# Delta-rule stages of a two-layer vision transformer on Trainium2: table switches, projections, inverse rows and the output product placed anew

## What is computed

```python
def step(S, inp):                       # one token; S is 16x16 for each head and image
    qt, kt, vt, at, gkt = inp
    Sp = S * jnp.exp(gkt)[..., None]
    u = jnp.einsum('bhk,bhkv->bhv', at, Sp) + vt
    S = Sp + jnp.einsum('bhk,bhv->bhkv', kt, u)
    o = jnp.einsum('bhk,bhkv->bhv', qt, S)
    return (S, o)
...
q, k, v = silu(x @ Wq), l2norm(silu(x @ Wk)), silu(x @ Wv)
log_f = jax.nn.log_sigmoid(x @ Wf)
gamma = -jax.nn.sigmoid(x @ Wgamma)
a = k * gamma * exp(log_f)
```

## Time and profile before

| what | value |
|---|---|
| median of 3 runs | 1997.47 us (1995.56 to 2000.2) |
| the profiled execution's own time | 1989.77 us |
| its span, first to last instruction | 1988.0 us |
| mean granted clock of TensorE | 0.857 |
| busy share of the span: TensorE, VectorE, ScalarE, GpSimd | 86%, 56%, 33%, 16% |
| first instruction of the delta stage k = 0 | 1303.05 us |
| start of k = 1, 2, 3 | 1321.4, 1348.1, 1392.3 us |
| start of k = 8, 9, 10 | 1687.3, 1743.8, 1789.5 us |
| first instruction after the last delta stage (ScalarE, L1324) | 1819.19 us |

### The profile page before, as it was taken

The page is one execution under the profiler, slowest core; times in us unless marked ns, Lnnn a source line. Parts: engine busy times, 40 slices in busy tenths (PEclk is TensorE's granted clock), DMA queues, the critical chain, the costliest instruction groups (busy, mean ns, idle before and its releaser), DMA issues. The chain is left out here.

```text
span 1988.0 us, 51796 instructions
## 1 busy us (share of the span) xinstructions
PE 1708.2 (86%) x22689; PEld 1517.3 (76%) x22689; DVE 1108.5 (56%) x2379; ACT 656.6 (33%) x1347; POOL 314.5 (16%) x284
## 2 busy tenths in 40 slices
PE   4677786799999999999999999876888888757589
PEld 4466675579988999989999999745877777756468
DVE  3655555674545555455555465566445555543885
ACT  3334534433322233232223232163333333223142
POOL 0232232520000000000000000052322223200530
PEclk9888988899999999999999999877666656655579
DMA  4100000100100000000101000100000000001001
GB/s 135 60 2 1 0 0 1 67 22 1 43 1 22 22 22 22 22 22 1 44 1 43 1 1 1 36 1 2 4 4 4 3 4 4 4 4 48 1 11 41
DMA packets 10070, 36.01 MB, mean 18 GB/s; under 512 B 3056, under 2 KB 6152, under 8 KB 7304
## 3 DMA queue, kind: packets, MB, share of 16 engines
q1 hardware_dynamic: 9864, 32.96, 4.8%
HBM read 30.47 MB, written 2.49 MB: 17 GB/s over the span
## 5 line engine op out<-in xcount | busy, mean ns | idle before, releaser
L1042 ACT ACTIVATE hidden<-bank,moe_b 128x512 f32<-128x512 f32 (+1 forms) x320 | 213.3, 668 | 537.1 <-PE bank L934 524.5
L951 PE MATMUL bank<-moe_w2h,hidden_hi 128*128 128x256 f32 x1216 | 345.7, 284 | 0.0
L951 PE MATMUL bank<-moe_w2l,hidden_hi 128*128 128x256 f32 x1216 | 344.0, 283 | 0.0
L951 PE MATMUL bank<-moe_w2h,hidden_lo 128*128 128x256 f32 x1216 | 343.9, 283 | 0.0
L934 PE MATMUL bank<-x_hi,moe_w1h 128*128 128x512 f32 (+1 forms) x640 | 243.8, 381 | 2.9 <-ACT hidden L1042 2.8
L934 PE MATMUL bank<-x_lo,moe_w1h 128*128 128x512 f32 (+1 forms) x640 | 242.5, 379 | 0.0
L934 PE MATMUL bank<-x_hi,moe_w1l 128*128 128x512 f32 (+1 forms) x640 | 242.0, 378 | 0.0
L951 PEld LDWEIGHTS bank<-moe_w2h,hidden_hi 128*128 128x128 f32 x1216 | 233.1, 192 | 6.0 <-DVE residual L1076 4.3
L1076 DVE SCALAR_TENSOR_TENSOR residual<-bank,gates,residual 128x256 f32<-128x256 f32 x152 | 73.4, 484 | 290.4 <-PE bank L951 290.4
L951 PEld LDWEIGHTS bank<-moe_w2l,hidden_hi 128*128 128x128 f32 x1216 | 233.2, 192 | 1.2
L951 PEld LDWEIGHTS bank<-moe_w2h,hidden_lo 128*128 128x128 f32 x1216 | 233.2, 192 | 0.0
(11 more groups left out here) (287 smaller groups left out, 3357.3 us busy)
## 6 DMA issues: line engine op xcount, KB each, us to landing
moe_w<-in_moe_w SPq DMA_DIRECT2D x16, 1024.0 KB, 4.8
patches<-in_patches SPq DMA_DIRECT2D x8, 864.0 KB, 4.6
out<-residual SPq DMA_DIRECT2D x19, 128.0 KB, 1.7
ffn_w<-in_ffn_w SPq DMA_DIRECT2D x2, 1024.0 KB, 6.4
att_w<-in_att_w SPq DMA_DIRECT2D x1, 1536.0 KB, 5.9
delta_w<-in_delta_w SPq DMA_DIRECT2D x1, 1280.0 KB
tok_w<-in_tok_w SPq DMA_DIRECT2D x1, 768.0 KB, 4.1
delta_wvf<-in_delta_wvf SPq DMA_DIRECT2D x1, 272.0 KB
```

The lines of the kernel that those rows point to most:

```text
L951: mm = nc.tensor.matmul(bank[4 + n % 3][:, 0:D], left, right, start=(i == 0), stop=(i == len(passes) - 1))
L1042: nc.scalar.activation(H[:, i % 4, 0:n], bank[i % 4][:, 0:n], ACT.Relu, bias=b1[:, x, f:f + 1]).then_inc(acted, 1)
```

## The change

Only `delta_stage` is changed.

- **ScalarE.** Three table loads a stage become two. Sigmoids come first, under one set: each value tile's Relu and Abs are followed at once by its sigmoid, then all four sigmoids of q and k. After `first_back(1)` comes the other set, then `forget_logs`, the two paddings and `inverse_norms`, ahead of the solution copies.
- **TensorE.** `project(0)` and `project(1)` stand right behind the values, `project(2)` and `project(3)` between the first halves. `key_norm(0)` and `key_norm(1)` move up behind `remainder(0)` and `remainder(1)`. `output` is called twice, with half of the lanes each; the first half goes into banks 2 and 3, the second into 0 and 1. `inverse_out(0)` moves ahead of `score(0)`, and `inverse_out(1)` ahead of `score(1)`.
- **VectorE.** All values and all silus come before row 5; `with_values(0)` before `log_forget`; rows 7 to 13 before the low parts of the output; `weigh(2)` and `weigh(3)` right behind row 15, `weigh(4)` and `weigh(5)` behind row 17, and the last two behind row 18.

```diff
@@ score, p == 0
-                        pe.wait_ge(o_lo, 2)
+                        pe.wait_ge(o_lo, 4)
@@ output
-            def output():
+            def output(j):
...
-                pe.wait_ge(u2_back, 4)
-                for p in range(IP):
+                pe.wait_ge(u2_back, 2 * (j + 1))
+                if j == 0 and c is not None:
+                    pe.wait_ge(v_out, 2)
+                for p in (2 * j, 2 * j + 1):
...
-                                    mm = nc.tensor.matmul(bank[s][32 * g:32 * g + 32, ts], UB[half(s), lane, :],
+                                    mm = nc.tensor.matmul(bank[2 - 2 * j + s][32 * g:32 * g + 32, ts], UB[half(s), lane, :],
@@ TensorE's list
             low_part(0)
             low_part(1)
-            first_half(0)
             project(0)
-            first_half(1)
             project(1)
             low_part(2)
-            remainder(0)
+            first_half(0)
             project(2)
             low_part(3)
-            remainder(1)
             project(3)
             low_part(4)
+            first_half(1)
+            remainder(0)
+            key_norm(0)
+            remainder(1)
+            key_norm(1)
             second_half(0)
             decay(0)
             second_half(1)
             decay(1)
-            key_norm(0)
-            key_norm(1)
-            output()
+            output(0)
             decay(2)
+            output(1)
+            inverse_out(0)
             score(0)
             decay(3)
-            inverse_out(0)
+            inverse_out(1)
+            score(1)
             decay(4)
-            score(1)
             decay(5)
-            inverse_out(1)
+            score(2)
             decay(6)
-            score(2)
             decay(7)
             inverse_out(2)
             score(3)
@@ ScalarE: high_out now takes (j, s), one copy of half the lanes for both m
-            nc.scalar.preload_act_table_set("natural_log_exp_and_others")
+            nc.scalar.preload_act_table_set("sigmoid_and_others")
             for p in range(IP):
                 forget_parts(p)
-            forget_logs()
-            nc.scalar.preload_act_table_set("sigmoid_and_others")
-            sigmoid_values(0)
-            sigmoid_values(1)
+                sigmoid_values(p)
+            sigmoid(0)
+            sigmoid(1)
             first_back(0)
-            sigmoid(0)
-            sigmoid_values(2)
-            first_back(1)
-            sigmoid(1)
-            sigmoid_values(3)
-            padded(0)
             sigmoid(2)
-            padded(1)
             sigmoid(3)
             for i in range(len(spans)):
                 low_high(i)
+            first_back(1)
             nc.scalar.preload_act_table_set("natural_log_exp_and_others")
+            forget_logs()
+            padded(0)
+            padded(1)
+            inverse_norms()
             solution(0)
             decay(0)
             solution(1)
             decay(1)
-            inverse_norms()
-            high_out(0)
-            high_out(1)
+            high_out(0, 0)
+            high_out(0, 1)
             decay(2)
+            high_out(1, 0)
+            high_out(1, 1)
+            inverse_back(0)
             decay(3)
-            inverse_back(0)
+            inverse_back(1)
             decay(4)
             decay(5)
-            inverse_back(1)
             decay(6)
             decay(7)
             inverse_back(2)
@@ VectorE: low_out takes (j, s) too, one subtraction; weigh waits for o_done 2
             for t in range(1, 5):
                 inverse_row(t)
-            log_forget()
-            inverse_row(5)
+            for p in range(IP):
+                values_of(p)
             silu_of(0)
-            values_of(0)
-            values_of(1)
             silu_of(1)
-            values_of(2)
-            values_of(3)
-            with_values(0)
             silu_of(2)
-            with_values(1)
             silu_of(3)
             gate_parts()
             step_scale()
-            for t in range(6, 10):
+            inverse_row(5)
+            with_values(0)
+            log_forget()
+            inverse_row(6)
+            bounded(0)
+            with_values(1)
+            bounded(1)
+            for t in range(7, 14):
                 inverse_row(t)
-            bounded(0)
-            bounded(1)
-            for t in range(10, 13):
-                inverse_row(t)
-            low_out(0)
-            low_out(1)
-            inverse_row(13)
+            for j in range(2):
+                for s in range(2):
+                    low_out(j, s)
             inverse_row(14)
             weigh(0)
             weigh(1)
             inverse_row(15)
+            weigh(2)
+            weigh(3)
             unit_key(0)
             unit_key(1)
             inverse_row(16)
-            weigh(2)
-            weigh(3)
             inverse_row(17)
+            weigh(4)
+            weigh(5)
             inverse_row(18)
-            for b in range(4, CB):
-                weigh(b)
+            weigh(6)
+            weigh(7)
```

More of the change, by code:

```diff
@@ L1616, in second_half @@
                 mm.then_inc(u2_done, 1)
-            def output():
+            def output(j):
                 if y is None:
                     return
-                pe.wait_ge(u2_back, 4)
-                for p in range(IP):
+                pe.wait_ge(u2_back, 2 * (j + 1))
+                if j == 0 and c is not None:
+                    pe.wait_ge(v_out, 2)
+                for p in (2 * j, 2 * j + 1):
                     for m in range(HALVES):
-                        ts = slice((IP * m + p) * SEQ, (IP * m + p + 1) * SEQ)
+                        ts = slice((2 * m + p % 2) * SEQ, (2 * m + p % 2 + 1) * SEQ)
                         for e in range(2):
@@ L1765, in padded, with high_out @@
                                      by_half(images(xl_c[:, m, nxt, :].bitcast(F32))), ACT.Copy).then_inc(in_lo, 1)
-            def high_out(s):
+            def high_out(j, s):
                 if y is None:
                     return
[L1770 to L1774, removed]
-            nc.scalar.preload_act_table_set("natural_log_exp_and_others")
+                act.wait_ge(o_done, j + 1)
+                nc.scalar.activation(
+                    xh_c[:, :, y].rearrange("p m (i s t) -> p s m i t", s=2, t=SEQ)[:, s, :, 2 * j:2 * j + 2],
+                    bank[2 - 2 * j + s][:, 0:4 * SEQ].rearrange("p (m i t) -> p m i t", m=HALVES, t=SEQ),
+                    ACT.Copy).then_inc(o_hi, 1)
+            nc.scalar.preload_act_table_set("sigmoid_and_others")
             for p in range(IP):
                 forget_parts(p)
-            forget_logs()
-            nc.scalar.preload_act_table_set("sigmoid_and_others")
-            sigmoid_values(0)
-            sigmoid_values(1)
+                sigmoid_values(p)
+            sigmoid(0)
+            sigmoid(1)
             first_back(0)
-            sigmoid(0)
-            sigmoid_values(2)
-            first_back(1)
-            sigmoid(1)
-            sigmoid_values(3)
-            padded(0)
             sigmoid(2)
-            padded(1)
             sigmoid(3)
@@ L1891, in weigh @@
                 if y is not None:
-                    dve.wait_ge(o_done, 1)
+                    dve.wait_ge(o_done, 2)
                 for e in range(2):
@@ L1910, in with_values, with low_out @@
                                         ALU.add).then_inc(rx_ready, 1)
-            def low_out(s):
+            def low_out(j, s):
                 if y is None:
                     return
[L1915 to L1921, removed]
+                dve.wait_ge(o_hi, 2 * j + s + 1)
+                low, high = (t[:, :, y].rearrange("p m (i s t) -> p s m i t", s=2, t=SEQ)[:, s, :, 2 * j:2 * j + 2]
+                             for t in (xl_c, xh_c))
+                nc.vector.tensor_tensor(
+                    low, bank[2 - 2 * j + s][:, 0:4 * SEQ].rearrange("p (m i t) -> p m i t", m=HALVES, t=SEQ),
+                    high.bitcast(F32), ALU.subtract).then_inc(o_lo, 1)
             def gate_parts():
```

## The result

The changed kernel takes **2077.22 us** (median of 4 runs, 2076.88 to 2078.39), against 1996.51 for the kernel before in the same comparison: ratio 1.0405, 95% interval 1.0385 to 1.0424. The forecast was 2082 and slower. The profiled execution took 2077.13 us (span 2075.4), 87.4 us more than the one before; the five full stages, 59.0 us long on average before and 72.6 after, hold 68 of them.

The account below looks back on a forecast made before the run. A full stage was taken as 40 us of TensorE's list, then 17 us of VectorE's. Five full stages at +13.2 us (+66) and the others summed to +84.6, giving 2074.4, plus 7.7: 2082 us, range 2052 to 2112.

Parts of the forecast that it names:

- wait before `key_norm(0)`: Full stage: TensorE waits for with_values(0), log_forget, two steps, clear and square after remainder(0), some 6.5 us.
- wait before `key_norm(1)`: Full stage: behind remainder(1), TensorE waits for GpSimd's clear_pairs(1) and square(1), 2.0 us.
- `score(0)` later in all: Full stage: score(0) was to start some 48 to 49 us into the stage, against 39.9 before.
- tail from `score(0)` on: Full stage: VectorE idle 3.6 us before weigh(2), and 2.45 against 1.55 before weigh(6); tail grows 4.5 us.
- Projections: Full stage: project(1), moved behind the values, falls into TensorE's high-clock stretch too, -0.7 us.
- Supply "as it is": TensorE's breaks in instruction supply, about 256 per 3.5 us, were left unchanged; bound 3 us either way.
- TensorE's work "the same otherwise": Full stage: apart from the projections' clock, TensorE's work was taken as unchanged.
- k = 1, +6 predicted: Stage k = 1, without lane work: key_norm(0) waits from the last projection through sigmoid, table, logs, steps and square, 6 us.
- The clock rival: New waits may remove TensorE's high-clock stretches, some 3.5 us a full stage, 3 each in k = 1 and 2; 2105 us; chance 0.15.
- Only the tail: Rival: front wait is refunded, adding some 2 us and not 9; full stage +6.5, whole 2038 us; chance 0.13.
- Faster: Rival: instruction supply bounds stages from k = 3 on and runs ahead during waits; 34 us gained, 1963 us; chance 0.04.
- The 7.7 us between profiled execution and median before: Added to the predicted profiled execution, 2074.4 us, because the earlier runs' median stood 7.7 above the profiled one.

Follow-up runs that it names:

- experiments 1 to 5: Changed kernel with GpSimd's squares first: 1.0204; scores first: 1.0184; both: 0.9957; log_forget ahead of with_values(0): 1.0377; score(3) ahead of inverse_out(2) alone: 1.0316.
- experiment 2: Changed kernel with score(1) ahead of inverse_out(1) and score(3) ahead of inverse_out(2) in TensorE's list: 2028.13 us, ratio 1.0184.
- experiment 1: Changed kernel with GpSimd doing square(0) and square(1) ahead of the steps and clears: 2034.56 us, ratio 1.0204.

## Why the prediction was right, step by step

| step, us per full stage | predicted | measured |
|---|---|---|
| wait before `key_norm(0)` | 6.5 | 6.14 |
| wait before `key_norm(1)` | 2.0 | 2.07 |
| `score(0)` later in all (five stages) | 8.7 | 9.0 (40.5 to 49.5) |
| idle before `weigh(2)` | 3.6 | 3.62 |
| idle before `weigh(6)` | 2.45 | 2.45 |
| tail from `score(0)` on | +4.5 | +4.7 (17.6 to 22.3; k = 6: +5.0) |
| full stage | +13.2 | +13.6 (59.0 to 72.6) |
| k = 1, 2, 8, 9 (windows above and the earlier trace rows) | +6, +9.5, +5.5, -1.4 | +7.8, +10.4, +4.1, -1.8 |
| span | +84.6 | +87.4 |

The mechanism was right in both places, and experiments 1 to 5 show each of them by itself. That the sum came out so close is luck in part: several terms inside it were off and nearly cancelled.

- **Projections, -0.7 predicted.** Behind the values three more projections fall into the high clock, not one. The window from 1637 to 1647 has a granted clock of 0.98, where the kernel before had 0.75 in the earlier trace rows. `project(1)` takes 0.93 us (1638.64 to 1639.57) after 1.73, and (2) and (3) 0.9 each after 1.8. With `project(0)` that is some 2.8 us less.
- **Supply "as it is".** The breaks grew from 3.1 to 3.8 us on the average of the full stages, in k = 6 from 2.8 to 4.8.
- **TensorE's work "the same otherwise".** Over the full stages the key norms, now two pieces, take 2.8 us after 2.0, the output in halves 3.7 after 2.9, and the values 5.4 after 4.8. These 2.2 us and the breaks took back what the projections gave; why each piece grew no run was made to show.
- **The tail.** The pair of unit keys takes 2.27 us beside GpSimd's steps in k = 6, and 0.85 in experiment 2, where no steps run beside it. The sum has no term for it; it was offset by row 16, whose multiplication stood beside GpSimd's steps in the kernel before (1.70 us in k = 6, 0.68 after).
- **k = 1, +6 predicted.** The wait is 6.22 us, but after it the clock is low: four norm matmuls take 2.40 us, 1.19 in the kernel before, and the stage's granted clock is 0.68 after 0.88.

The clock rival was wrong for the full stages: the new waits come after the high stretch, which got longer. In k = 6 the granted clock is 1.00 from 1636.3 to 1646.5 and 0.50 from there on, before the wait begins at 1648.6; with the wait gone (experiment 1) it falls at the same place, 1.00 from 1609.1 to 1619.3 of a stage that starts at 1599.5 and then 0.50. In k = 1 it holds, and the rule of the Trainium skill (TensorE: Matmul & The Clock Gate, HAM oscillation), an idle gap brings the low clock, agrees there; in the full stages the kernel before had the low clock without any gap. "Only the tail" fell with experiment 1: the front wait was paid for with 40 us. "Faster" fell too: in k = 6 breaks of 2.07 and 1.23 us come after waits of 6.14 and 2.07, so the supply did not run ahead by the length of a wait. The 7.7 us between profiled execution and median before did not carry over: 2077.13 and 2077.22 after. So the forecast, 4.8 us above the measured time, is a sum that was 2.8 us short and 7.7 us added that were not there.

## What to carry to other kernels

In a kernel of hand-written lists, take each instruction that moves and ask what the third engine does before it gives what is waited for: here a list of GpSimd that nobody had touched made 8 us of every full stage. A load that is saved gains nothing where it was covered already, while two lines in the order of a waiting engine cost or give 2%. And never let an engine's product stand behind work that itself waits for the engine which wants that product.

## What the runs showed of the hardware

The breaks named "issue" on TensorE come in a measure of 256 instructions, matmuls and weight loads counted together. In the delta stages the traces of before and after have 34 and 38 breaks over 0.25 us, and every distance from one to the next is a multiple of 256 instructions to within one. Between the last two in k = 6 of the changed kernel, 1671.66 and 1675.51, lie one matmul with its load, one decay (6) and 124 matmuls with their loads (248): 256 instructions in 3.85 us, and 128 matmuls of a lane product with their loads, 256 too, take 1.7 to 2.3. Two breaks that are 256 instructions apart are never less than 3.47 us apart in these two traces, 3.31 in all thirteen. The Trainium skill (Advanced Engine Details and Errata, ISA Cache) gives two lines of 256; that even a wait of 6 us doesn't buy more than the next line fits it: 2.07 and 1.23 us of breaks follow in the same stage. That the breaks are the filling of such lines stays an inference, and the refill time as such no run measured by itself.
